# Stores of the edge sort spread over more stages, self loops beside a matrix product, and tables of the last layer in one run per lane

## The chip, the cores and the metric

The kernel runs on one core of one Trainium2 chip. The metric is the device time of one execution in microseconds (us). Engines are named as in the profile: PE is TensorE (matmul), DVE VectorE, ACT ScalarE, POOL GpSimd, SP SyncE, which here only issues transfers.

## What is computed

A graph network on 3125 nodes of 64 features and 100,000 edges that are sorted by target. Four layers follow each other, each as `x = layernorm(x + layer(x))`:

```
x = LN(x + L0(x, edges, 4))            # four normalised sums over neighbours
x = LN(x + L1(x, src, dst, ...))       # edge MLP gives a gate; sum and max per target; node MLP
x = LN(x + L2(x, edges, ...))          # three convolutions with self loops
x = LN(x + L3(x, relations, edges, edge_type))

def L3(e, ...):                        # two hops, head = src, tail = dst
    res = e
    for _ in range(2):
        e = l2_normalize(agg(e, relations, head, tail, type))   # mean over each head's edges
        res = 0.5 * res + e
    return res
```

The last layer sums by source. So the edges must be sorted once more, by source, before it begins.

## The kernel before

Nodes lie as 25 blocks of 128 in the first three layers and as 33 blocks (`SB`) of 96 (`BN`) in the last one. The program is a chain of stages. Each stage is a call of `drive`, which gives every engine its own program, and between two stages stands a barrier of all engines (L111, L113): the next stage begins when the last engine is through, POOL's queue of transfers included (the instruction DRAIN at L111).

**Sorting by source.** `sort_places` computes for each edge its row in the sorted table and keeps rows and edge codes in DRAM as 28 batches of 28 columns (`K.queue`). The 784 stores that carry them out are indirect transfers of 128 edges each, issued by POOL at L445 in `place_batches` and called placements below. SP brings each batch into one of two buffers (`queue_batches`, L430) after waiting until the placements of the batch two before it have landed. The placements of a stage are paced: after every `stored` of them POOL waits for one more increment of `pace`, a semaphore of that stage's own work. They go beside this other work: 224 in the stage that builds the pair matrix (`build_pairs`), 280 in the stage of the first layer's hops (`Pairs.hops`, paced by `full[0]`, 6 at a time), the rest in `dense` calls of later layers and in the second layer's loops.

**Stages around the change**, in the order of time: "steps" and "bases" compute tables of the second layer's edge loop and of node degrees (L516 to L640 and L768 on); then `build_pairs`; then `hops`, where PE and DVE run four rounds over 25 blocks and SP first stores the pair matrix (L1072); then the fetch of weights, the first `dense` of the second layer, and its edge loop. `merge` (L1655 to L1672) joins maximum and sum of the messages on DVE, while POOL adds self loops to the pair matrix (`with_loops`, L862, 25 instructions; they follow the matrix's load). Two `dense` calls of the node MLP follow, the first with batch 18.

**The last layer.** `steps3` turns the sorted edges into lists of ids with matmuls (L1923): DVE prepares `local`, `where`, `half`, `odd` and `kind`, and one semaphore, `selected`, lets PE begin. `edge_loop3` runs once per hop. Its start (`nodes_first`) makes the table `tab3` of 3168 rows of 66 values in SBUF, SP stores it (L2126), and then POOL gathers 68 tiles of tail rows in each of 12 steps (L2158, 1632 gathers in both hops); DVE, ACT and PE work on what was gathered. In the second hop the residual mix is computed at L2430 and stored (L2129). `mix_in` loads it and the layer's input (L2011, L2012), and POOL halves and adds them (L2030, L2033) before DVE's final sum and norm (L2045).

In `by_block`, the layout of both tables before, node n is row n, so that one of the 96 lanes holds rows n, n+96, n+192 and so on: 33 separate runs of 264 bytes for `tab3` and of 256 bytes for `mix`.

## Time and profile before

| what | us |
|---|---|
| runs | 5718.30, 5718.80, 5719.78 (median 5718.8) |
| profiled execution, its own time | 5712.27 |
| its span | 5710.5 |
| busy: DVE, POOL | 3715.3, 3453.4 |
| busy: PE matmul, PE weight load, ACT | 2917.1, 2314.5, 1759.2 |
| POOL: 1632 gathers of the last layer, busy | 1699.1 |
| POOL: 784 placements, busy | 807.9 |

The profile is of one execution. Busy shares are averages over some forty stages with different limits, so they tell little about a change that touches eight of them; the timeline and the waits inside a stage do. In rows of a timeline the first number is the start in us from the span's start, the second the duration; the bracket says how long the engine stood idle before and what released it, and "issue" there is time in which it waited for nothing the profile shows. A row "POOL L445" is a placement's work on POOL, not its landing in DRAM.

### The profile page before, as it was taken

Reading aid. Unit: us, or ns where it says so; the run is one execution under the profiler, and the core shown is the slowest. Engines: PE = TensorE matmul, PEld = TensorE weight load, DVE = VectorE, ACT = ScalarE, POOL = GpSimd, SP = SyncE. Lnnn points to the kernel's source line nnn. Section 1 sums busy time; section 2 is a strip of 40 time slices with the busy share of each in tenths; the row PEclk is TensorE's granted clock in tenths of the full one; section 3 lists DMA queues with packets and bytes.
Section 4 is the critical chain, followed back from the end, with each engine's and each line's share of the span. In section 5 each row is a group of like instructions: output and inputs, shape, how many; then the busy total and the mean of one; then the engine's idle time right before and its main releaser. Section 6 shows DMA issues by size and latency. Waiting matters only on the chain. (4 is left out here: it accounts for less than half of the span.)

```text
span 5710.5 us, 76336 instructions
## 1 busy us (share of the span) xinstructions
PE 2917.1 (51%) x18212; PEld 2314.5 (41%) x18213; DVE 3715.3 (65%) x6539; ACT 1759.2 (31%) x5177; POOL 3453.4 (60%) x3383
## 2 busy tenths in 40 slices
PE   4344578724555555264736426455564244555543
PEld 1233456514454444143424225444453234444443
DVE  4645554306777777233332569899998579998987
ACT  0055500001111111110010035655654146556552
POOL 4077337737777777432613477777772577777771
PEclk7655589956666666566857655556655556665655
DMA  6031040027777777500000212222220321222211
GB/s 214 31 106 52 0 142 2 2 79 205 217 214 221 214 216 203 173 9 0 4 7 9 53 42 58 45 54 50 50 46 7 68 54 44 55 49 50 53 32 18
DMA packets 491952, 449.20 MB, mean 79 GB/s; under 512 B 135374, under 2 KB 439172, under 8 KB 491667
## 3 DMA queue, kind: packets, MB, share of 16 engines
q1 hardware_dynamic: 257963, 232.05, 14.7%
q0 software_dynamic: 116768, 136.51, 10.3%
q10 hardware_dynamic: 116936, 77.08, 4.2%
q8 instruction: 149, 2.44, 0.2%
q14 instruction: 136, 1.11, 0.1%
HBM read 308.22 MB, written 137.16 MB: 78 GB/s over the span
## 5 line engine op out<-in xcount | busy, mean ns | idle before, releaser
L2158 POOL DMA_INDIRECT tg<-tab_d,tail_ids x1632 | 1699.1, 1041 | 543.3 <-issue 494.6
L445 POOL DMA_INDIRECT sorted_edges_d<-place_batch x784 | 807.9, 1030 | 749.6 <-DMA place_batch<-place_queue_d 340.0
L2197 PE MATMUL acc<-msg,sum_hot 128*96 128x65 f32 x3264 | 547.0, 366 | 961.0 <-ACT msg L2271 748.5
L2197 PEld LDWEIGHTS acc<-msg,sum_hot 128*96 128x96 f32 x3264 | 529.4, 279 | 976.9 <-issue 976.9
L1494 POOL DMA_INDIRECT xg<-tab_d,src_i x784 | 767.7, 979 | 252.3 <-issue 238.5
L2187 PE MATMUL hr<-near_table,near_hot 128*128 x4896 | 679.2, 266 | 197.2 <-DVE near_hot L2319 95.0
L2187 PEld LDWEIGHTS hr<-near_table,near_hot 128*128 128x128 f16 x4896 | 497.4, 105 | 380.5 <-issue 281.8
L2246 ACT ACTIVATE pr<-hr 128x396 f32<-128x396 f32 x576 | 277.8, 483 | 590.9 <-PE hr L2187 584.7
L2260 ACT ACTIVATE msg<-tg,coef_b 128x64 f32<-128x64 f32 x1632 | 396.6, 334 | 31.3 <-DVEq L2667 31.3
L1508 PE MATMUL hq<-ex,sameU 128*128 128x128 f32 x1568 | 269.2, 350 | 260.5 <-DVEq L1613 194.4
L2487 DVE TENSOR_REDUCE scal<-prod 128x17 f32<-128x1088 f32 x288 | 370.5, 1286 | 9.9
L1508 PEld LDWEIGHTS hq<-ex,sameU 128*128 128x128 f32 x1568 | 262.3, 265 | 275.8 <-issue 275.8
L2266 ACT ACTIVATE pr<-pr,coef_c 128x64 f32<-128x64 f32 x1496 | 365.4, 334 | 0.0
L717 PE MATMUL ring<-step_cells,step_lows 128*128 128x200 f16 x1184 | 229.6, 374 | 232.3 <-DVE step_lows L695 95.6
L906 PE MATMUL aggps<-shared,pair_m 128*128 128x192 bf16 (+1 forms) x1800 | 263.0, 286 | 80.4 <-DVEq L934 65.8
L717 PEld LDWEIGHTS ring<-step_cells,step_lows 128*128 128x128 f16 x1184 | 174.9, 157 | 287.0 <-issue 286.2
L2311 DVE TENSOR_TENSOR scal<-scal 128x68 f32<-128x68 f32 (+1 forms) x1272 | 264.3, 245 | 28.2 <-ACT scal L2251 9.3
L1611 DVE TENSOR_TENSOR h<-hq,xg 128x1792 f32<-128x1792 f32 x56 | 113.4, 2025 | 212.2 <-DMA xg<-tab_d,src_i 206.8
L695 DVE TENSOR_TENSOR step_lows<-low_rows,room 128x1024 f16<-128x1024 f16 x148 | 102.6, 693 | 222.5 <-PE ring L717 222.1
L906 PEld LDWEIGHTS aggps<-shared,pair_m 128*128 (+1 forms) x1800 | 176.1, 99 | 167.3 <-issue 97.5
L1546 ACT ACTIVATE back<-bk 128x896 f32<-128x896 f32 x112 | 102.8, 918 | 443.2 <-PE bk L1518 443.2
L2311 DVE TENSOR_TENSOR prod<-pr,tg 128x1088 f32<-128x1088 f32 x96 | 124.3, 1295 | 169.4 <-DMA tg<-tab_d,tail_ids 166.5
(469 smaller groups left out, 5402.5 us busy)
## 6 DMA issues: line engine op xcount, KB each, us to landing
ex<-spread_d SPq DMA_DIRECT2D x112, 448.0 KB, 5.5
msg_d<-back ACTq DMA_DIRECT2D x112, 448.0 KB
near_hot<-head_row_d SPq DMA_DIRECT2D x96, 408.0 KB
tg<-tab_d,tail_ids POOLq DMA_INDIRECT x1632
spread_d<-zeros ACTq DMA_DIRECT2D x28, 896.0 KB, 10.9
spread_d<-zeros SPq DMA_DIRECT2D x28, 896.0 KB, 8.8
idsU<-dst_short_d SPq DMA_DIRECT2D x112, 224.0 KB, 6.6
pairs_d<-pair_m SPq DMA_DIRECT2D x3, 4800.0 KB
```

Of the source, the lines that this page charges most:

```text
L445: l.eng.indirect_dma_start(K.sorted_edges[:, :], bass.IndirectOffsetOnAxis(ap=K.batch[:, n % 2, 0, k:k + 1], axis=0), K.batch[:, n % 2, 1, ...
L717: e.matmul(banks[:, bass.ds(regs[k], KW)], lows[s][:, :, k], cells[s][:, k, :], start=False, stop=False, skip_group_check=True).then_inc(s ...
L906: ins = l.eng.matmul(ps[s][:, 0:3 * w], self.m[:, b, bass.ds(at, P)], parts[:, b, :], start=b == 0, stop=b == NB - 1)
L1494: l.eng.indirect_dma_start(xg[j.c % ROWS][:, half * H + k, :], None, K.tab1, bass.IndirectOffsetOnAxis(ap=src_i[:, t:t + 1], axis=0)).then ...
L1508: ins = e.matmul(hq[:, k, :], same[j.slot][:, k, :], ex[j.slot][:, k, :], start=True, stop=True)
L2158: e.indirect_dma_start(tg[:, u % TAILS * GQ + k, :], None, K.tab3, bass.IndirectOffsetOnAxis(ap=K.tail_ids[:, u * GQ + k:u * GQ + k + 1], ...
L2187: ins = e.matmul(hr[(u * FILLS + g) % 2][:, c:c + PW3], near_hot[u % HOTS][:, k, :], rows[:, bass.ds(at[k] + n * PW3, PW3)], start=n == 0, ...
L2197: ins = e.matmul(sums[:, bass.ds(at[k], D + 1)], sum_hot[u % 2][:, k, :], msg[u % QN][:, k, :], start=False, stop=False, skip_group_check= ...
L2260: a.activation(msg[u % QN][:, k, 0:D], tg[:, tails(u).start + k, 0:D], ACT.Copy, scale=kB[s][:, t.start + k:t.start + k + 1]).then_inc(tai ...
L2266: a.activation(r, r, ACT.Copy, scale=kC[s][:, k:k + 1]).then_inc(kinds_scaled, 1)
L2311: tt_ = lambda o, x, y, op: v.tensor_tensor(o, x, y, op).then_inc(l.sem, l.add(1))
L2487: v.tensor_reduce(sc[:, n, q * GQ:(q + 1) * GQ], prod[q % 2][:, :, :], AX.X, ADD).then_inc(l.sem, l.add(1))
```

## The change

1. Placements are spread otherwise. Batch 0 goes into the stage "steps" and batch 1 into "bases", both unpaced; batches 2 to 9 into `build_pairs` as before; batches 10 to 16 into `hops` (196 in place of 280, 4 for each increment), two of them fetched ahead of the pair matrix's stores; batch 17 into the first `dense` of the second layer.
2. `with_loops` leaves `merge` and runs on POOL beside the node MLP's second `dense`; its half identity takes the room of the first `dense`'s weights.
3. `tab3` lies by lane: lane p's 33 rows follow each other, so its store is one run of 8712 bytes per lane. Tail ids are recomputed to match: n becomes (n mod 96)*33 + n div 96, by five more DVE instructions in `steps3`; `selected` is raised twice.
4. `mix` lies by lane too. The second hop halves its value once more and adds half of the input, so that `mix_in` loads one array and needs nothing from POOL.

```
-def place_batches(l, K, first, count, pace, stored):
+def place_batches(l, K, first, count, pace=None, stored=BATCH):
...
-            if done and done % stored == 0:
+            if pace is not None and done and done % stored == 0:
@@ steps
+            place_batches(l, K, 0, 1)
...
+            queue_batches(l, K, 0, 2)
@@ build_pairs
-            place_batches(l, K, 0, 8, turned, 4)
+            place_batches(l, K, 2, 8, turned, 4)
@@ node_bases
+        place_batches(l, K, 1, 1)
@@ Pairs.hops
+                queue_batches(l, self.K, 10, 2)
                 for c0, c1 in self.columns:
                     l.eng.dma_start(cells[:, :, c0:c1], self.m[:, :, c0:c1]).then_inc(kept, 16)
-                queue_batches(l, self.K, 8, 10)
+                queue_batches(l, self.K, 12, 5)
...
-                place_batches(l, self.K, 8, 10, full[0], 6)
+                place_batches(l, self.K, 10, 7, full[0], 4)
@@ second layer
-        dense(nc, K, tabs[:, :, :], [(K.x[:, :, :], wab[:, :])], bab[:, :])
+        dense(nc, K, tabs[:, :, :], [(K.x[:, :, :], wab[:, :])], bab[:, :], batches=(17, 1))
...
-    drive(nc, "merge", dict(vector=vector, gpsimd=gpsimd))
+    drive(nc, "merge", dict(vector=vector))
     dense(nc, K, h2, [(mm, wn1a), (K.x[:, :, :], wn1b)], bn1, relu=True, room=droom, batches=(18, 1))
-    dense(nc, K, o, [(h2, wn2)], bn2, room=droom)
+    dense(nc, K, o, [(h2, wn2)], bn2, room=droom, beside=loops)
@@ steps3, vector
+            v.tensor_scalar(half[:, :, :], tail[:, :, :], 2731, None, ALU.mult).then_inc(l.sem, l.add(1))
+            v.tensor_scalar(odd[:, :, :], tail[:, :, :], SB, None, ALU.mult).then_inc(l.sem, l.add(1))
+            settle()
+            for c in range(QC):
+                v.scalar_tensor_tensor(chosen[:, c, :], steps16[:, :], first[:, c:c + 1], begun[:, c, :], ALU.is_gt, ALU.mult).then_inc(l.sem, l.add(1))
+            settle()
+            v.sem_inc(selected, 1)
+            v.tensor_scalar(half[:, :, :], half[:, :, :], 18, None, ALU.logical_shift_right).then_inc(l.sem, l.add(1))
+            settle()
+            v.scalar_tensor_tensor(tail[:, :, :], half[:, :, :], float(1 - SB * BN), odd[:, :, :], ALU.mult, ALU.add).then_inc(l.sem, l.add(1))
@@ steps3, tensor
+                    if h == 0 and j == 2:
+                        e.wait_ge(selected, 2)
@@ mix_in
-        s.dma_start(mix[:, :, :], by_block(K.mix)).then_inc(loaded, 16)
-        s.dma_start(x[:, :, :], by_block(K.xd)).then_inc(loaded, 16)
+        s.dma_start(x[:, :, :], K.mix.rearrange("p (b f) -> p b f", f=D)).then_inc(loaded, 16)
...
-        l.eng.tensor_scalar(mix[:, :, :], mix[:, :, :], 0.5, None, ALU.mult).then_inc(l.sem, l.add(1))
...
-        l.eng.tensor_tensor(x[:, :, :], x[:, :, :], mix[:, :, :], ALU.add).then_inc(added, 1)
@@ edge_loop3
-        q.dma_start(by_block(K.tab3), tab).then_inc(tails_stored, 16)
+        q.dma_start(by_lane(K.tab3), tab).then_inc(tails_stored, 16)
...
-                v.scalar_tensor_tensor(mix[:, :, :], mix[:, :, :], 0.5, ev, ALU.mult, ALU.add).then_inc(l.sem, l.add(1))
+                v.scalar_tensor_tensor(sq, mix, 0.5, ev, ALU.mult, ALU.add).then_inc(l.sem, l.add(1))
             settle()
             v.sem_inc(heads_tabled, 1)
+            if hop == 1:
+                v.scalar_tensor_tensor(mix, sq, 0.5, mix, ALU.mult, ALU.add).then_inc(l.sem, l.add(1))
+                settle()
+                v.sem_inc(mixed, 1)
```

How the order of instructions moves is shown at three places. The first is POOL from the stage "steps" to the first `dense` of the second layer, the difference in two pieces (`sorted_edges_d` is the sorted table, `place_batch` the two buffers of a batch; L111, L113 and L162 are the barrier and the start of a stage's program):

```order
 L552 IOTA count_f 128x1184
+L445 DMA sorted_edges_d<-place_batch 100352x1 x28
 L111 UNCONDITIONAL_BRANCH
 L113 ISA x2
 L162 UNCONDITIONAL_BRANCH
-L783 IOTA node_ids 128x3208
+L785 IOTA node_ids 128x3208
+L445 DMA sorted_edges_d<-place_batch 100352x1 x28
 L111 UNCONDITIONAL_BRANCH
```

```order
-L445 DMA sorted_edges_d<-place_batch 100352x1 x280
+L445 DMA sorted_edges_d<-place_batch 100352x1 x196
 L111 UNCONDITIONAL_BRANCH
-L113 ISA x8
+L113 ISA x6
 L162 UNCONDITIONAL_BRANCH
```

POOL had nothing but one IOTA in each of the first two stages; now each holds 28 placements behind it, and the stage of the hops holds 84 fewer.

The second is SP in the stage of the hops, before:

```order
L1072 DMA pairs_d<-pair_m 128x25x768 x3
L1072 DMA pairs_d<-pair_m 128x25x832
L430 DMA place_batch<-place_queue_d 128x56 x10
L111 UNCONDITIONAL_BRANCH
```

and of the change:

```order
L430 DMA place_batch<-place_queue_d 128x56 x2
L1076 DMA pairs_d<-pair_m 128x25x768 x3
L1076 DMA pairs_d<-pair_m 128x25x832
L430 DMA place_batch<-place_queue_d 128x56 x5
L111 UNCONDITIONAL_BRANCH
```

Two batches are now fetched ahead of the four stores of the pair matrix, and five behind.

The third is DVE in `steps3`, before:

```order
L1865 TENSOR_SCALAR begun_1<-steps_3_1,last_step_1 112x944 x7
L1866 TENSOR_SCALAR kind_1<-kind_1 112x896
L1867 TENSOR_SCALAR half_1<-tail_1 112x896
L1868 TENSOR_SCALAR odd_1<-tail_1 112x896
L1871 SCALAR_TENSOR_TENSOR chosen_1<-steps_3_1,first_step_1,begun_1 112x944 x7
L1872 TENSOR_SCALAR kind_1<-kind_1 112x896
L1873 CAST half_1<-half_1 112x896
L1874 CAST odd_1<-odd_1 112x896
L1880 TENSOR_TENSOR off_1<-colps_1,count_1 128x408
```

and of the change:

```order
L1877 TENSOR_SCALAR half_1<-tail_1 112x896
L1878 TENSOR_SCALAR odd_1<-tail_1 112x896
L1881 SCALAR_TENSOR_TENSOR chosen_1<-steps_3_1,first_step_1,begun_1 112x944 x7
L1884 TENSOR_SCALAR half_1<-half_1 112x896
L1886 SCALAR_TENSOR_TENSOR tail_1<-half_1,odd_1 112x896
L1888 TENSOR_SCALAR half_1<-tail_1 112x896
L1889 TENSOR_SCALAR odd_1<-tail_1 112x896
L1891 CAST half_1<-half_1 112x896
L1892 CAST odd_1<-odd_1 112x896
L1893 TENSOR_SCALAR kind_1<-kind_1 112x896
L1899 TENSOR_TENSOR off_1<-colps_1,count_1 128x408
```

Before, PE was released behind L1874; now it is released once behind L1881 and a second time, for `half` and `odd`, behind L1893.

## Rows read from the trace of the kernel before

**Rows 1.** Windows: stretch, length, busy PE PEld DVE ACT POOL, PEclk, DMA, GB/s.

```profile
760.00:1117.00 357.00, 320.97 (x2477) 233.79 (x2478) 140.00 (x575) 0.00 (x0) 239.28 (x250) 1.00 0.14 39
1117.00:1170.00 53.00, 0.42 (x6) 0.20 (x3) 14.48 (x24) 0.00 (x0) 32.57 (x31) 0.54 0.02 3
```

**Rows 2.** Timeline of the hops' stage: first and last placement, DVE's end, next stage.

```profile
798.10 0.95 POOL L445 DMA_INDIRECT sorted_edges_d<-place_batch  x1 [170.12 <-DMA place_batch<-place_queue_d]
...
1130.82 1.82 DVE L1135 TENSOR_TENSOR nodes<-nodes,col_b 128x1600 f32<-128x1600 f32 x1
...
1157.76 0.96 POOL L445 DMA_INDIRECT sorted_edges_d<-place_batch  x1 [0.30 <-issue]
1164.95 0.17 DVE L1408 MEMSET bab<- 128x128 f32 x1 [32.31 <-PEq L113]
```

**Rows 3.** Timeline, first dense of the second layer: DVE's eleventh group, next stage's start.

```profile
1209.57 0.69 DVE L1256 TENSOR_TENSOR tabs<-dop,bab 128x512 f32 x1 [2.67 <-PE dop L1240]
...
1216.72 0.18 DVE L1326 TENSOR_SCALAR has<-degree 128x25 f32<-128x25 f32 x1 [1.30 <-PEq L113]
```

**Rows 4.** Timeline, node MLP's first dense: last placement, start of the next stage.

```profile
2450.42 0.96 POOL L445 DMA_INDIRECT sorted_edges_d<-place_batch  x1 [0.30 <-issue]
...
2457.96 0.63 ACT L1213 ACTIVATE spare<-B 128x512 f32 x1 [6.03 <-PEq L113]
```

**Rows 5.** Timeline: POOL's first instruction of the stages bases and build_pairs.

```profile
198.12 2.81 POOL L783 IOTA node_ids<- 128x3208 f32 x1 [53.95 <-SPq L111]
...
274.51 0.30 POOL L669 IOTA cell_row<- 128x200 f32 x1 [73.58 <-POOLq L113]
```

**Rows 6.** Timeline of merge (POOL, DVE), and the start behind the second dense.

```profile
2365.92 17.59 POOL L862 TENSOR_TENSOR pair_m<-pair_m,spare 128x128 f16<-128x128 f16 x18 [0.28 <-POOL spare L1669]
...
2374.67 3.60 DVE L1664 TENSOR_TENSOR B<-B,has_edges 128x3200 f32<-128x3200 f32 x1
...
2386.29 2.60 POOL L862 TENSOR_TENSOR pair_m<-pair_m,spare 128x128 f16<-128x128 f16 x7 [2.78 <-DMA pair_m<-pairs_d]
...
2484.70 1.82 DVE L1678 SCALAR_TENSOR_TENSOR B<-nodes,B 128x1600 f32<-128x1600 f32 x1 [1.29 <-PEq L113]
```

**Rows 7.** Timeline of steps3: an integer operation of two inputs, DVE's last, PE's first.

```profile
3136.41 1.08 DVE L1859 SCALAR_TENSOR_TENSOR local<-block,head 112x896 f16<-112x896 int32 x1
...
3152.82 0.62 DVE L1874 CAST odd<-odd 112x896 f16<-112x896 int32 x1
...
3153.65 2.54 PE L1923 MATMUL colps<-chosen,local 112*128 112x408 f16 x7 [52.58 <-DVEq L1876]
```

**Rows 8.** Timeline, first hop: the table's store and the first gather.

```profile
3209.85 0.32 SPq L2126 DMA_DIRECT2D tab_d<-pr  x1
...
3220.13 0.99 POOL L2158 DMA_INDIRECT tg<-tab_d,tail_ids  x1 [16.30 <-DMA tab_d<-pr]
```

**Rows 9.** Windows of 2 us: the table's store early and late, the mix's store.

```profile
3211.00:3213.00 2.00, 0.00 (x0) 0.00 (x0) 2.00 (x1) 0.00 (x0) 0.00 (x0) 0.50 1.04 189
...
3215.00:3217.00 2.00, 0.00 (x0) 0.00 (x0) 1.97 (x2) 0.00 (x0) 0.00 (x0) 0.50 1.01 86
4472.00:4474.00 2.00, 2.00 (x5) 0.46 (x3) 2.00 (x4) 0.00 (x0) 1.39 (x3) 0.50 0.83 201
```

**Rows 10.** Page's part 5 and waits for tile tg: the gathers, who waited for them.

```profile
L2158 POOL DMA_INDIRECT tg<-tab_d,tail_ids x1632 | 1699.1, 1041 | 543.3 <-issue 494.6
...
  DVE prod L2311: 166.5, 28
```

**Rows 11.** Timeline, second hop: the mix on DVE and the gather beside it.

```profile
4468.89 2.35 DVE L2430 SCALAR_TENSOR_TENSOR pr<-pr 96x2112 f32<-96x2112 f32 x1
4470.02 2.04 POOL L2158 DMA_INDIRECT tg<-tab_d,tail_ids  x1 [0.30 <-issue]
```

**Rows 12.** Timeline of mix_in: POOL's first operation, DVE's start behind its second.

```profile
5677.76 5.55 POOL L2030 TENSOR_SCALAR mix<-mix 96x2112 f32<-96x2112 f32 x1 [41.99 <-DMA x<-x_kept_d]
...
5688.15 1.29 DVE L2045 TENSOR_TENSOR x<-x,e 96x1088 f32<-96x1088 f32 x1 [10.45 <-POOL x L2033]
```

More of the change, by code:

```diff
@@ L471, in keep_common @@
     K.pairs = dr("pairs", [NP * PW, 1], F16)
-    K.xd, K.mix = (dr(n, [NP, D], F32) for n in ("x_kept", "mix"))
+    K.xd, K.mix = dr("x_kept", [NP, D], F32), dr("mix", [BN, SB * D], F32)
     K.tab1, K.qtab = dr("tab1", [NP, D + P], F32), dr("qtab", [NP, P], F32)
@@ L1171, with dense @@
 TH = T // 2
-def dense(nc, K, out, pieces, bias=None, relu=False, room=None, batches=None):
+def dense(nc, K, out, pieces, bias=None, relu=False, room=None, batches=None, beside=None):
     width = out.shape[2]
@@ L1271, in dense @@
             programs.update(sync=sync, gpsimd=gpsimd)
+        if beside is not None:
+            programs.update(gpsimd=beside)
         drive(nc, "dense", programs)
@@ L1639, in finish1 @@
     droom = spare[:, 0:2048]
-    half = spare[:, 0:P // 2].bitcast(F16)
     at = 2048
@@ L1646, in finish1 @@
     wn1a, wn1b, wn2, bn1, bn2, mid = views
+    half = wn1a[:, 0:P // 2].bitcast(F16)
     L, R = slice(0, D), slice(D, P)
@@ L1665, in vector, with loops @@
         l.eng.wait_ge(l.sem, l.done())
-    def gpsimd(l):
-        e = l.eng
-        e.tensor_scalar(half, K.ident[:, :], 0.5, None, ALU.mult).then_inc(l.sem, l.add(1))
-        e.wait_ge(l.sem, l.done())
-        e.sem_inc(l.sink, 1)
+    def loops(l):
+        l.eng.tensor_scalar(half, K.ident[:, :], 0.5, None, ALU.mult).then_inc(l.sem, l.add(1))
+        l.eng.wait_ge(l.sem, l.done())
+        l.eng.sem_inc(l.sink, 1)
         pairs.with_loops(l, half)
-    drive(nc, "merge", dict(vector=vector, gpsimd=gpsimd))
+    drive(nc, "merge", dict(vector=vector))
     dense(nc, K, h2, [(mm, wn1a), (K.x[:, :, :], wn1b)], bn1, relu=True, room=droom, batches=(18, 1))
-    dense(nc, K, o, [(h2, wn2)], bn2, room=droom)
+    dense(nc, K, o, [(h2, wn2)], bn2, room=droom, beside=loops)
     def vector(l):
@@ L1783, in by_block, with by_lane @@
     return rows[0:SB * BN, :].rearrange("(b p) f -> p b f", p=BN)
+def by_lane(rows):
+    return rows.rearrange("(p b) f -> p b f", p=BN)
 def steps3(nc, K):
@@ L1869, in vector @@
             settle()
-            for c in range(QC):
-                v.scalar_tensor_tensor(chosen[:, c, :], steps16[:, :], first[:, c:c + 1], begun[:, c, :], ALU.is_gt, ALU.mult).then_inc(l.sem, l.add(1))
-            v.tensor_scalar(kind16[:, :, :], kind[:, :, :], float(BN), None, ALU.add).then_inc(l.sem, l.add(1))
             v.tensor_copy(half16[:, :, :], half[:, :, :]).then_inc(l.sem, l.add(1))
             v.tensor_copy(odd16[:, :, :], odd[:, :, :]).then_inc(l.sem, l.add(1))
+            v.tensor_scalar(kind16[:, :, :], kind[:, :, :], float(BN), None, ALU.add).then_inc(l.sem, l.add(1))
             settle()
@@ L1920, in tensor @@
                 for j, xs in enumerate(((local16,), (where16,), (half16, half16, odd16))):
+                    if h == 0 and j == 2:
+                        e.wait_ge(selected, 2)
+                        e.sem_inc(l.sink, 1)
                     for n, x in enumerate(xs):
@@ L2002, in mix_in @@
     sb = lambda n, s, d: st.enter_context(nc.sbuf_tensor(fresh(n), s, d))
-    e, sq, x, mix = (sb(n, [BN, SB, D], F32) for n in ("e3", "sq3", "x3", "mix3"))
+    e, sq, x = (sb(n, [BN, SB, D], F32) for n in ("e3", "sq3", "x3"))
     counts = sb("counts3", [BN, SB], F32)
     mean, var = sb("mean3", [BN, SB], F32), sb("var3", [BN, SB], F32)
-    loaded, squared, added, centred, mixed, stored = (st.sem(fresh(n)) for n in ("loaded", "squared", "added_x", "centred", "mixed", "stored"))
+    loaded, squared, centred, mixed, stored = (st.sem(fresh(n)) for n in ("loaded", "squared", "centred", "mixed", "stored"))
     halves = [slice(0, 17), slice(17, SB)]
@@ L2025, in scalar @@
             l.eng.activation(sq[:, at, :], x[:, at, :], ACT.Square).then_inc(squared, 1)
-    def gpsimd(l):
-        l.eng.wait_ge(loaded, 32)
-        l.eng.sem_inc(l.sink, 1)
-        l.eng.tensor_scalar(mix[:, :, :], mix[:, :, :], 0.5, None, ALU.mult).then_inc(l.sem, l.add(1))
-        l.eng.wait_ge(l.sem, l.done())
-        l.eng.sem_inc(l.sink, 1)
-        l.eng.tensor_tensor(x[:, :, :], x[:, :, :], mix[:, :, :], ALU.add).then_inc(added, 1)
     def vector(l):
@@ L2041, in vector @@
         entities(v, l, acc, e, sq, squared, counts[:, :], a, b, t)
-        v.wait_ge(added, 1)
+        v.wait_ge(loaded, 16)
         for at in halves:
@@ L2061, in vector @@
         v.wait_ge(mixed, 2)
-    drive(nc, "mix", dict(sync=sync, scalar=scalar, gpsimd=gpsimd, vector=vector))
+    drive(nc, "mix", dict(sync=sync, scalar=scalar, vector=vector))
 def edge_loop3(nc, K, st, table, relation, acc, hop):
@@ L2101, in edge_loop3 @@
     keyed = [st.sem(fresh(f"keyed{r}")) for r in range(HOTS)]
-    squared, rooted, kinds_last = sem("squared"), sem("rooted"), sem("kinds_last")
+    squared, rooted, kinds_last, mixed = sem("squared"), sem("rooted"), sem("kinds_last"), sem("mixed3")
     (shaped, cleared, near_made, near_full, near_taken, coefs, tails_scaled, kinds_scaled, summed, positive, sum_made, added, asked, answered) = (
@@ L2125, in sync @@
         q.wait_ge(tails_tabled, 1)
-        q.dma_start(by_block(K.tab3), tab).then_inc(tails_stored, 16)
+        q.dma_start(by_lane(K.tab3), tab).then_inc(tails_stored, 16)
         if hop == 1:
-            q.wait_ge(heads_tabled, 1)
-            q.dma_start(by_block(K.mix), mix).then_inc(mix_stored, 16)
+            q.wait_ge(mixed, 1)
+            q.dma_start(K.mix.rearrange("p (b f) -> p b f", f=D), mix).then_inc(mix_stored, 16)
         for u in range(HOTS, QUARTERS):
```

3 lines of the change are left out of this document (2 added, 1 removed).

## The prediction

> **What bounds the kernel now.** I read the busy shares first, to see that no engine is full throughout, and then the kernel stage by stage: since a barrier ends each stage, what counts is which engine comes last in it. The windows show the hops' rounds bound by PE (320.97 us of 357, POOL 239.28), and then 53 us in which PE works 0.42, DVE 14.48 and POOL 32.57 [rows 1]: POOL alone holds the stage. The timeline says how long: DVE's last instruction ends at 1132.64, the last placement at 1158.72, and the next stage starts at 1164.95 [rows 2], 6.23 after it, since POOL's queue is drained before the barrier. Where DVE ends a stage, the next starts 1.30 later [rows 3]. So three stages end with POOL's work while DVE is through: the hops, `merge` and `mix_in`. In the last layer POOL is the pace: its 1632 gathers take 1699.1 us and it stands idle 543.3 around them, of which 494.6 is the 0.30 of issuing each; the rest is mostly the wait for each hop's table (16.30 in the first [rows 8]). DVE waits for gathered rows 166.5 us [rows 10]. What starts the gathers earlier therefore ends the hop earlier.
>
> **The change part by part**, against the profiled execution's 5712.27 us.
>
> *The hops' stage.* 84 of 280 placements leave it. Before, the first one ran at 798.10, after 170.12 idle for its batch, since the fetch stood behind the pair matrix's stores on SP [rows 2]. Now two batches are ahead of these stores, and 196 placements at 4 for each increment need 49 groups. The increments come about every 6.87 us (357 us by 52 of them), four placements cost 4 x 1.26 = 5.0 (0.96 and 0.30 each [rows 2]), so POOL waits for each increment and places its last group near 760 + 48 x 6.87 = 1090, ends near 1095 and is drained near 1100. That is before DVE, which ends at 1132.64 as it did, so the next stage starts at 1132.64 + 1.30 = 1133.94 and not at 1164.95: **-31.0**. Bounds: -31.0, and -24 if the end of DVE comes later because POOL's stores now crowd the start, which the trace speaks against (PE and not DVE is the bound there, DVE 140.00 of 357 [rows 1]).
>
> *The first dense of the second layer* takes 28 of them, 4 after each of 6 increments of `done[0]`. The sixth comes with the eleventh group, whose sum on DVE starts at 1209.57 [rows 3]. The last four placements end near 1209.4 + 5.1 = 1214.5. Then comes the drain: 6.23 from the last placement to the next stage in the hops [rows 2], 6.58 in the one dense that already has a batch (2451.38 to 2457.96 [rows 4]). That gives 1220.8 in place of 1216.72: **+4.2**. Bounds 0 (the drain is hidden) and +6 (the placements lag one group).
>
> *Steps and bases* take 28 placements each. POOL's next instruction after the first comes at 198.12, after 53.95 idle, and after the second at 274.51, after 73.58 idle [rows 5]. 28 placements cost 28 x 1.26 = 35.3, or 28 x (1.93 + 0.30) = 62 if each ran as slowly as a gather beside a two-input DVE operation (2.04 [rows 11]). With 6.2 for the drain this is 41.5 or at worst 68: in bases it fits into the 73.6 idle, in steps 41.5 fits into 53.95 and 68 doesn't, but the two-input operations of DVE fill a small part of that stage. I take **0**, bounds 0 and +6; without that cover the cost would be 41.5 a stage. The pair matrix's stage keeps its 224 placements: 0.
>
> *merge.* DVE ends at 2378.27, POOL's additions at 2388.89, because the last seven wait for the matrix's load [rows 6]. Without them the stage ends with DVE: **-10.5**, bounds -9 and -11.5. They cost 17.59 for 18 beside DVE and 2.60 for 7 alone [rows 6], so 10 to 25 us with the half identity, beside a dense that runs from 2457.96 to 2484.70 less the barrier, 25.4 us [rows 4, 6]. They fit, and the load has landed by then: 0, bound +1. Batch 18 is now fetched some 10 us earlier, beside the end of the matrix's load; its placements are paced by the dense, which hides a late start unless it is over 5 us.
>
> *steps3.* PE starts at 3153.65, 0.2 behind DVE's last of `kind`, `half` and `odd` (0.62 each, overlapping to 1.6 in all [rows 7]). These now stand behind the release: **-1.6**. The new chain (0.62, 1.08, 1.15 for `half` and `odd`, 1.7 for the casts and `kind`, by [rows 7]) takes some 4.6, and PE has `local` with 2.54 and `where` with about as much before it needs them. Bounds -1.6 and +0.5.
>
> *The tables.* The store is issued at 3209.85 and the first gather starts at 3220.13, after 16.30 idle for it [rows 8]. The data flow at 189 GB/s at first and at 86 near the end, while the mix's rows of 256 bytes ran at 201 [rows 9]. At 201 the 0.84 MB need 4.2 us and not the 6.2 that I read; one run per lane should do no worse and may do better, 3 us. I take **-3.2 in each hop**, nearer to the fast row since the tail at 86 goes, bounds 0 and -5. In the Trainium skill, "DMA: Bandwidth & Descriptors", Specifications, full rate wants transfers of at least 512 bytes. By that the mix's 256-byte rows should be as slow as the table's 264, and [rows 9] show them at over twice the late rate, so the measurement decides and the gain may be smaller than the rule suggests.
>
> *The second hop's extra operation* costs 2.35 on DVE like the one at L2430, which DVE wins back while it waits for gathers. The gather beside that one took 2.04 where another took 0.99 [rows 8, 11]: **+1.1** on POOL. Bounds 0 and +2.4.
>
> *mix_in.* POOL begins at 5677.76, as the second load lands. DVE is ready at 5688.15 - 10.45 = 5677.70 and waits 10.45 for POOL's two operations [rows 12]. These go. The stage's loads begin about 10 us earlier, so one load with half of the bytes lands before DVE is ready: **-10.4**, bounds -8 and -10.5.
>
> SP's two more fetches in steps stand ahead of the loads of that stage: +0.3.
>
> **Sum**: -31.0 + 4.2 - 10.5 - 1.6 - 3.2 - 3.2 + 1.1 - 10.4 + 0.3 = -54.3, so 5712.3 becomes 5658.0. The median of the runs lies 6.5 above the profiled execution, and the next runs are as likely to lie there: 5718.8 - 54.3 = **5664.5**. About 0.2%, 11.4 us, is what a measurement of this kernel tells from no change.
>
> **Rivals.**
>
> *The gathers become slower (the other side).* They are the pace of 24 steps, so what each gains in length counts 1632 times. To be slower than before by 0.2% the 54.3 must be lost and 11.4 more: 65.7 / 1632 = 0.040 us each, from a mean of 1.041 to 1.081 [rows 10]. If they came to 1.09, the time would be 5664.5 + 80 = 5745. For it: the table's rows lie in another order, and a gathered tile's rows with it. Against it: the duration on POOL is that of writing descriptors, whose number and size stay, and ids are random in either layout. Chance 3%.
>
> *POOL holds back DVE in the two early stages.* A placement writes descriptors while DVE runs operations of two inputs; the rows show the gather delayed (2.04) and DVE's 2.35 unchanged [rows 11]. If it went the other way, each of 14 long operations of the two stages would wait up to one placement, 0.96: +13, 5678. In the Trainium skill, "GPSIMD Engine Reference", Key points, POOL shares its memory interfaces with DVE in such operations; it speaks against putting stores there, but doesn't say who wins. The trace so far has DVE winning. With the case that POOL outlasts steps (+6, 5670.5) chance 12%.
>
> *The table's store doesn't get faster.* Its late rate could come from something else, such as queues that finish at different times. Then 6.4 are missing: 5671. Chance 20%.
>
> *The hops' gain doesn't come in full.* If the increments come later than I read, or the batches 12 to 16 still wait behind the pair matrix's stores, POOL lags. 112 placements behind a first one at 798 need only 141 us, so it would have to lag by over 30 us more than before. If it did, half of the 31 would be missing: 5680. Chance 5%.
>
> **How the numbers follow.** The forecast has 60%, within it 5655 to 5672 by the bounds of the dense (-4 to +2), the tables (-4 to +6) and the early stages. The rivals at 5671 and 5678 belong to the faster side too. For 8 in 10 I reach from 5652 to 5680. Faster by over 0.2% holds the forecast and the last three rivals, less 2 in 100 for a slowing of the gathers that only eats the gain: 0.95; same 0.02, slower 0.03 from the first rival.
>
> **What would show it.** Right: the next stage behind the hops starts 1.3 us after DVE's last instruction, with POOL's last placement near 1095; `merge` ends with DVE; the idle time before the first gather shrinks from 16.30 by some 3 us; DVE in `mix_in` has no wait of 10 us; the first dense's next stage starts some 4 us later. Wrong: gathers of a mean above 1.05, a stage steps or bases that ends with POOL, placements still running past 1132, or a table store that takes as long.

## The result and the profile after

| what | before | changed |
|---|---|---|
| runs, us | 5718.30 to 5719.78, median 5718.8 | 5662.21, 5667.17, 5668.14, median 5667.17 |
| profiled execution, us | 5712.27 | 5667.17 |
| ratio of the runs, 95% interval | | 0.9915 [0.9902, 0.9929] |

The kernel became 51.6 us faster by the medians, against 54.3 forecast (5664.5). The profiled executions differ by 45.1: that of before lay 6.5 below its kernel's median, that of the change on it. What follows is worked out between these two, stage by stage, and then tested.

The page of the changed kernel (span, busy times, and the two groups of part 5 that concern the change):

```profile
span 5665.4 us, 76347 instructions
...
PE 2926.1 (52%) x18212; PEld 2321.6 (41%) x18213; DVE 3718.3 (66%) x6544; ACT 1759.1 (31%) x5177; POOL 3474.6 (61%) x3381
...
L2171 POOL DMA_INDIRECT tg<-tab_d,tail_ids x1632 | 1713.4, 1050 | 532.9 <-issue 495.6
L445 POOL DMA_INDIRECT sorted_edges_d<-place_batch x784 | 834.0, 1064 | 858.9 <-DMA place_batch<-place_queue_d 352.4
```

The averages say little: the engines' busy shares moved by a hundredth at most. One number matters later: the gathers take 1.050 us in the mean and not 1.041 [rows 10], which is 14.3 us over all 1632 (1713.4 against 1699.1).

| stage | forecast, us | by the two timelines, us |
|---|---|---|
| to the end of "steps" | +0.3 | +3.25 |
| "bases", `build_pairs` | 0 | +0.2, +1.5 |
| the hops' stage | -31.0 | -30.5 |
| first dense of the second layer | +4.2 | +1.75 |
| `merge` | -10.5 | -11.2 |
| node MLP's two dense calls | 0 | -0.3 |
| steps3 to PE's first matmul | -1.6 | -1.7 |
| table, first and second hop | -3.2, -3.2 | -5.0, -5.5 |
| from first gather to the end of the hop, first and second | 0, +1.1 | +3.0, +10.6 |
| `mix_in` | -10.4 | -10.35 |

What is missing to -45.1 is about -1 in stages that the change doesn't touch.

**The hops** (timeline of the changed kernel: last placement, DVE's last instruction, next stage's first):

```profile
1098.46 0.96 POOL L445 DMA_INDIRECT sorted_edges_d<-place_batch  x1 [0.31 <-issue]
...
1135.71 1.83 DVE L1139 TENSOR_TENSOR nodes<-nodes,col_b 128x1600 f32<-128x1600 f32 x1
1139.38 0.17 DVE L1414 MEMSET bab<- 128x128 f32 x1 [1.84 <-PEq L113]
```

The last placement ends at 1099.42, 38 us before DVE, and the next stage starts 1.84 behind DVE; before, it started 6.2 behind the last placement [rows 2]. The whole tail of POOL is gone. The stage itself began 4.9 later than before.

**The first dense** (last placement, DVE's last, next stage):

```profile
1188.51 0.95 POOL L445 DMA_INDIRECT sorted_edges_d<-place_batch  x1 [0.30 <-issue]
1189.52 0.42 DVE L1260 TENSOR_TENSOR tabs<-dop,bab 128x256 f32<-128x256 f32 x1 [1.38 <-PE dop L1244]
...
1192.98 0.18 DVE L1332 TENSOR_SCALAR has<-degree 128x25 f32<-128x25 f32 x1 [3.04 <-PEq L113]
```

DVE ends at 1189.94, and the next stage starts 3.04 behind it instead of 1.30 [rows 3]. POOL's last placement ended at 1189.46, so 3.5 us pass between it and the next stage, not the 6.2 to 6.6 that I forecast. The 6.58 of [rows 4] was a misreading. In that dense, too, four placements stood at the end behind a pause, but DVE had one more operation to do:

```profile
2454.24 1.83 DVE L1261 TENSOR_SCALAR B<-B 128x3200 f32<-128x3200 f32 x1
```

It ended at 2456.07, and the next stage started 1.89 behind it: DVE ended that stage, and the 6.58 is no price of POOL's. By the records of the instruction DRAIN itself, POOL was through 4.63 us after the last placement in the hops of the kernel before, and 2.48 after it in that dense; in the new dense it is 2.36. A drain isn't a fixed price: here it was longer behind the long unbroken row of stores than behind four.

**Steps** (SP's last load, DVE's first operation on loaded data, DVE's last, next stage):

```profile
149.66 2.01 SPq L566 DMA_DIRECT2D before_i<-in_dst_dram  x3
...
156.35 0.63 DVE L574 TENSOR_SCALAR group_i<-step_raw 112x896 int32<-112x896 int32 x1 [11.17 <-DMA before_i<-in_dst_dram]
...
199.42 0.55 DVE L620 SCALAR_TENSOR_TENSOR room<-stepps,count_f 1x392 int32<-1x392 f32 x1
201.37 2.81 POOL L785 IOTA node_ids<- 128x3208 f32 x1 [16.66 <-SPq L111]
```

Before, DVE's first operation on loaded data came earlier:

```profile
153.29 0.63 DVE L572 TENSOR_SCALAR group_i<-step_raw 112x896 int32<-112x896 int32 x1 [8.31 <-DMA before_i<-in_dst_dram]
```

DVE waits 11.17 us for the last load, and 8.31 before. Everything behind is shifted by that: from that operation to DVE's last it takes 43.6 us, and 43.4 before, and its seven `chosen` operations take 9.63 in both kernels. POOL's placements didn't slow DVE; the loads landed later. How much later varies: e3 and e4 below have the same early stages, and there the wait was 9.29 and 8.76.

**merge and the loops** (DVE's last of `merge`, the next stage's first, and POOL's additions in their new place):

```profile
2351.34 3.49 DVE L1670 TENSOR_TENSOR B<-B,has_edges 128x3200 f32<-128x3200 f32 x1
...
2355.91 0.42 ACT L1217 ACTIVATE spare<-B 128x256 f32 x1 [67.52 <-PEq L113]
...
2424.36 7.70 POOL L865 TENSOR_TENSOR pair_m<-pair_m,spare 128x128 f16<-128x128 f16 x20 [0.28 <-POOL spare L1674]
```

DVE now ends `merge` (2354.83), and the 25 additions run beside the second dense in 9.5 us altogether; the dense takes 26.9 us, and 26.7 before [rows 6].

**steps3** (PE's first, DVE's last conversion, PE's first matmul on `half`):

```profile
3115.57 2.54 PE L1945 MATMUL colps<-chosen,local 112*128 112x408 f16 x7 [50.89 <-DVEq L1883]
...
3119.57 0.62 DVE L1893 TENSOR_SCALAR kind<-kind 112x896 f16<-112x896 int32 x1
...
3120.39 3.03 PE L1945 MATMUL colps<-chosen,half 112*128 112x408 f16 x14
```

PE starts 4.6 us ahead of the end of DVE's chain, which is done at 3120.19, just before PE needs it at 3120.39. The margin is 0.2 us.

**The tables** (the store and the first gather of hop one, the first gather of hop two; then the first two windows of 2 us of the store, columns as in [rows 9]):

```profile
3171.99 0.30 SPq L2139 DMA_DIRECT2D tab_d<-pr  x1
...
3177.26 1.19 POOL L2171 DMA_INDIRECT tg<-tab_d,tail_ids  x1 [11.28 <-DMA tab_d<-pr]
...
4413.07 1.25 POOL L2171 DMA_INDIRECT tg<-tab_d,tail_ids  x1 [24.78 <-DMA tab_d<-pr]
```

```profile
3173.00:3175.00 2.00, 0.00 (x0) 0.00 (x0) 2.00 (x1) 0.00 (x0) 0.00 (x0) 0.50 0.97 274
3175.00:3177.00 2.00, 0.00 (x0) 0.00 (x0) 1.97 (x2) 0.00 (x0) 0.00 (x0) 0.50 0.19 78
```

The wait falls from 16.30 to 11.28 [rows 8]. The data flow at 274 GB/s in the first of these windows and are through in the second; the slow end at 86 [rows 9] is gone. **mix_in** (the one load, and DVE's sum, which waits for nothing; it came at 5688.15 behind a wait of 10.45 [rows 12]):

```profile
5632.59 0.30 SPq L2033 DMA_DIRECT2D x<-mix_d  x1
...
5643.03 1.29 DVE L2058 TENSOR_TENSOR x<-x,e 96x1088 f32<-96x1088 f32 x1
```

### The profile page after: what moved, and what is told of

It is laid out like the page before. It is cut to its first block and busy times, and to the rows that moved or that the text cites. A ratio compares the mean times of both kernels' runs of the same rounds, so it can differ in the third digit from the quotient of the medians.

```text
span 5665.4 us, 76347 instructions
## 1 busy us (share of the span) xinstructions
PE 2926.1 (52%) x18212; PEld 2321.6 (41%) x18213; DVE 3718.3 (66%) x6544; ACT 1759.1 (31%) x5177; POOL 3474.6 (61%) x3381
## 5 line engine op out<-in xcount | busy, mean ns | idle before, releaser
L2171 POOL DMA_INDIRECT tg<-tab_d,tail_ids x1632 | 1713.4, 1050 | 532.9 <-issue 495.6
L445 POOL DMA_INDIRECT sorted_edges_d<-place_batch x784 | 834.0, 1064 | 858.9 <-DMA place_batch<-place_queue_d 352.4
```

The costliest lines, as they stand in the source:

```text
L445: l.eng.indirect_dma_start(K.sorted_edges[:, :], bass.IndirectOffsetOnAxis(ap=K.batch[:, n % 2, 0, k:k + 1], axis=0), K.batch[:, n % 2, 1, ...
L2171: e.indirect_dma_start(tg[:, u % TAILS * GQ + k, :], None, K.tab3, bass.IndirectOffsetOnAxis(ap=K.tail_ids[:, u * GQ + k:u * GQ + k + 1], ...
```

## The experiments

Theory: each part brings what its stage shows, and the 9 us by which the profiled execution misses the forecast (45.1 against 54.3) lie in the gathers. Rivals: the layout by lane makes gathers slower; the added operation does; or hops vary from run to run. All kernels start from the changed one. Runs on one chip are compared with each other; e1 to e4 ran on one (there the kernel before took 5706.28 to 5718.59, median 5714.13, 9 runs), e5 to e8 and e9 to e12 on two others.

### e1: the stores of the sort as before

```
-            place_batches(l, K, 0, 1)
...
-            queue_batches(l, K, 0, 2)
...
-        place_batches(l, K, 1, 1)
...
-            place_batches(l, K, 2, 8, turned, 4)
+            place_batches(l, K, 0, 8, turned, 4)
...
-                queue_batches(l, self.K, 10, 2)
...
-                queue_batches(l, self.K, 12, 5)
+                queue_batches(l, self.K, 8, 10)
-                place_batches(l, self.K, 10, 7, full[0], 4)
+                place_batches(l, self.K, 8, 10, full[0], 6)
...
-        dense(nc, K, tabs[:, :, :], [(K.x[:, :, :], wab[:, :])], bab[:, :], batches=(17, 1))
+        dense(nc, K, tabs[:, :, :], [(K.x[:, :, :], wab[:, :])], bab[:, :])
```

> The spread of the sort's stores is undone, all else is as in the change. Theory A (POOL's tail alone held the hops' stage; the early stages pay 4.6 us, of which 3.1 is the later landing of a load in the stage steps, and the first dense 1.8): 30.5 - 4.6 - 1.8 = 24 us slower than the change, near 5691, with 5 us less before the hops' stage and the next stage 31 us behind DVE's end again. Theory B (stores are better spread because the memory queues are less crowded in the hops): more than 35 us slower. If the last layer's gathers keep their 1.050 us here, the spread of stores has nothing to do with their slowing.

Measured: 5693.71 (5685.05 to 5696.81), ratio 0.9962 [0.9949, 0.9976] to the kernel before, against 0.9915 for the change: 0.47%, some 27 us. The next stage behind the hops starts behind POOL again:

```profile
1165.30 0.17 DVE L1410 MEMSET bab<- 128x128 f32 x1 [33.57 <-PEq L113]
```

The stage took 425.7 us (424.6 before), steps and bases were back at 57.0 and 76.3, `build_pairs` at 465.8, the dense at 44.86. Here "steps" is counted from the stage's first instruction to the next stage's first; the kernel before has 57.4, the change 60.4. So the spread of stores is worth 30.5 - 1.75 - 4.7 = 24, as theory A says. It alone pays ahead of the hops, but not always 4.7: on this chip the hops began at 739.6 (e1) and 740.0 (e2) without it, and at 742.7 (e3) and 741.1 (e4) with it.

### e2: ten batches in the hops, two of them fetched ahead

```
-                queue_batches(l, self.K, 10, 2)
+                queue_batches(l, self.K, 8, 2)
...
-                queue_batches(l, self.K, 12, 5)
+                queue_batches(l, self.K, 10, 8)
-                place_batches(l, self.K, 10, 7, full[0], 4)
+                place_batches(l, self.K, 8, 10, full[0], 6)
```

with steps, bases and the first dense as in e1.

> All ten batches stay in the hops' stage as before the change, 6 for each increment, but two are fetched ahead of the pair matrix's stores; steps, bases and the first dense have none. Theory A (what held the hops was the first placement's start at 798, not the number: 280 x 1.26 = 353 us from about 762 end at 1115, drained near 1120, ahead of DVE's end): 6 us faster than the change, near 5661, since steps and the first dense give their 4.6 and 1.8 back. Theory B (with every increment used up the placements run past DVE's end at 1132.6, because a collision with DVE's norm or a late batch costs them more): within 10 us of the change on either side, POOL last in the stage.

Measured: 5663.43 (5655.85 to 5666.58), ratio 0.9911 [0.9897, 0.9924]. The last placement and the next stage:

```profile
1113.30 0.96 POOL L445 DMA_INDIRECT sorted_edges_d<-place_batch  x1 [0.30 <-issue]
...
1134.56 0.17 DVE L1411 MEMSET bab<- 128x128 f32 x1 [1.85 <-PEq L113]
```

280 placements are done at 1114.26, 18 us before DVE. The stage took 394.6, as with the change (394.1), and the early stages and the dense had their times of before. e1 and e2 differ in nothing but the place of this fetch, and their medians lie 30.3 us apart. So on this chip what held the hops was the late first placement, 170 us idle for a batch behind the pair matrix's stores, and not the number of stores. Whether fewer stores without the earlier fetch are enough as well wasn't tried here. On this chip one line on SP's queue is worth as much as the whole spread. As a time a gain over the change isn't shown: the intervals overlap.

### e3: the table by block; e4: the mix as before

e3 takes `by_block(K.tab3)` and the ids, DVE's order and the single release of before; e4 takes `mix_in` of before and

```
-                v.scalar_tensor_tensor(sq, mix, 0.5, ev, ALU.mult, ALU.add).then_inc(l.sem, l.add(1))
+                v.scalar_tensor_tensor(mix[:, :, :], mix[:, :, :], 0.5, ev, ALU.mult, ALU.add).then_inc(l.sem, l.add(1))
...
-            if hop == 1:
-                v.scalar_tensor_tensor(mix, sq, 0.5, mix, ALU.mult, ALU.add).then_inc(l.sem, l.add(1))
-                settle()
-                v.sem_inc(mixed, 1)
```

> The last layer's table by block as before, ids unconverted, the rest as in the change. Theory A (store and steps3 gave 5.0 + 5.5 + 1.7, and the gathers' 1.050 against 1.041 us is a pattern of collisions that has nothing to do with the layout): 12 us slower than the change, near 5679, gathers anywhere between 1.04 and 1.055. Theory B (rows by lane make the gathers slower, 0.009 x 1632 = 14 us): gathers back at 1.041, time within 4 us of the change.

> The residual mix as before: two arrays loaded at the end, halved and added on POOL, no second operation on DVE in the second hop. Theory A (10.4 at the end, 1.1 on the gathers of the second hop): 9 us slower than the change, near 5676. Theory B (the added operation on DVE shifts the steps against the gathers and is what made the second hop 10.6 us longer): about as fast as the change, and the second hop's 816 gathers span 1097 us as before the change in place of 1108.

Measured: e3 5675.99 (5674.14 to 5680.66), ratio 0.9940 [0.9926, 0.9953]; e4 5666.44 (5652.46 to 5671.60), ratio 0.9922 [0.9908, 0.9936]. e3 loses what its stages say: the first gathers come 9.2 and 9.3 us behind their stores, not 5.3 and 5.2, PE's first matmul in steps3 comes 1.5 later, and `mix_in` keeps its gain. Its gathers did not return to 1.041: the mean was 1.050 and 1.045 in the two hops. The layout isn't what slows them. e4 is the surprise. At `mix_in` it loses its gain (DVE waits 10.85 us for POOL again), yet its median is that of the change. The rows of tile `tg` (minimum, median, maximum in ns) show why, for the kernel before, the change, e3 and e4:

```profile
L2158 POOL DMA_INDIRECT tg<-tab_d,tail_ids x1632: 940/944/2970, 3220.1 to 5555.9; - x182
```

```profile
L2171 POOL DMA_INDIRECT tg<-tab_d,tail_ids x1632: 942/952/2807, 3177.3 to 5521.5; - x182
```

```profile
L2159 POOL DMA_INDIRECT tg<-tab_d,tail_ids x1632: 942/952/2764, 3183.3 to 5528.3; - x182
```

```profile
L2180 POOL DMA_INDIRECT tg<-tab_d,tail_ids x1632: 940/944/2819, 3166.7 to 5496.0; - x182
```

The median gather takes 944 ns before and in e4, 952 in the change and in e3 (also in e1 and e2). All 1632 together took 1699.1 us before and 1697.7 in e4, but 1713.4 in the change and 1709.5 to 1716.3 in e1 to e3. So some 14 us are lost, but the step of the median isn't all of it: of the gathers up to 1.1 us the mean moved by 3 ns only, from 966 to 969, which is less than 5 us; the rest lies in those over 1.1 us (343.9 us before, 361.3 in the change, eight more of them). Both theories for e4 fell as put: the second hop is not alone (its 816 gathers spanned 1098.8 us, the first hop's 1093.7; with the change 1108.4 and 1100.0), and the price isn't 1.1 us. By these profiles the new mix gives 10.35 at the end and takes about as much in the gathers of both hops. In times that isn't settled: e4's interval also holds the 9 us of theory A. And its profiled execution was the fastest of its five, 14 us below their median; its first gather came 10.6 us earlier than the change's, in stages that are the same in both. One of them, the second layer's edge loop, took 1048.0 us in the change and 1041.2 in e4.

### e5 to e8: a second chip

e5 is the change itself, e6 the kernel of e2, e7 moves the two fetches of "steps" behind the stage's loads, and e8 undoes both e3's and e4's parts.

```
         def sync(l):
             e = l.eng
-            queue_batches(l, K, 0, 2)
...
                 e.dma_start(out, ends(t0, t1), allow_slow_non_contiguous=True).then_inc(loaded, 16)
+            queue_batches(l, K, 0, 2)
```

> The change itself, run beside the next three. The profiles so far show each stage within 0.5 us of its price but the 1632 gathers between 1094 and 1108 us a hop. Theory A (the length of a hop varies from execution to execution, whatever the kernel): the two hops' gathers come out differently from the 1100 and 1108 of the change's first profile, by up to 8 us, and the rest of the stages the same within 1 us. Theory B (the change's layout or its second operation sets it): again 1100 and 1108 within 2 us.

> The kernel with ten batches in the hops, two of them fetched ahead, once more beside the change. Its stages promise 4.6 + 1.8 = 6.4 us less than the change. Theory A (the stages add up): 4 to 8 us below the change in the medians. Theory B (variation of the hops hides it): within 3 us.

> In the stage steps the two batches are fetched behind the stage's own loads instead of ahead of them. Theory A (the 3.1 us of that stage are the last load's landing, late because fetches and placements share the memory queues with it): DVE's first shift on loaded data starts 8.3 us after its cast, as before the change, and the stage is 3 us shorter; POOL ends near 190 and is drained before DVE is through. Theory B (placements slow DVE's own operations): the stage stays 3 us longer than before the change. Theory C (POOL now outlasts the stage): 1 to 5 us longer than the change.

> The last layer is as before the change in all its parts (table by block, ids unconverted, mix by two inputs), the early stages as in the change. By the stages 5.0 + 5.4 + 1.7 + 10.3 - 1.1 = 21.3 us slower than the change, less what the gathers gain. Theory A (variation of executions): gathers of a hop span anything from 1094 to 1108. Theory B (the change's last layer makes them slower): both spans within 1 us of 1097, and the kernel only 7 to 10 us slower than the change.

| kernel | median, us | to the kernel before (7547.02, 11 runs) |
|---|---|---|
| e5, the change | 7382.83 | 0.9786 [0.9766, 0.9806] |
| e6, ten ahead | 7457.81 | 0.9898 [0.9873, 0.9923] |
| e7, loads first | 7390.01 | 0.9793 [0.9774, 0.9813] |
| e8, last layer as before | 7407.91 | 0.9817 [0.9797, 0.9836] |

This chip runs every kernel a third slower. DVE's, ACT's and POOL's instructions last as long as on the first; the loops' engines stand idle more, in time that the profile puts to "issue" or to a release it doesn't show. Gathers no longer set the pace there, so the spans of 816 say nothing and the theories for e5 can't be told apart. Three readings hold all the same. In e7 DVE's first operation on loaded data waits 8.44 us for its loads, in e5 10.30:

```profile
152.50 0.63 DVE L574 TENSOR_SCALAR group_i<-step_raw 112x896 int32<-112x896 int32 x1 [8.44 <-DMA before_i<-in_dst_dram]
```

```profile
154.62 0.63 DVE L574 TENSOR_SCALAR group_i<-step_raw 112x896 int32<-112x896 int32 x1 [10.30 <-DMA before_i<-in_dst_dram]
```

Fetching behind the loads gives the stage its early start back, as before the change (8.31). Yet the stage became 10 us longer: 69.2 against 58.8 in e5. DVE waited twice, 6.4 and 8.3 us, for results of PE (the profile names no releaser), and PE's weight loads came mostly one at a time, each behind a pause in which it waited for nothing that the profile shows:

```profile
191.88 0.10 PEld L634 LDWEIGHTS stepps<-chosen,cell 112*128 112x128 f16 x1 [1.18 <-issue]
...
194.01 0.10 PEld L634 LDWEIGHTS stepps<-chosen,where 112*128 112x128 f16 x1 [1.29 <-issue]
```

This lasted until about 197.5, as POOL's placements (the last ended at 194.7) and its drain (197.5) did. So none of the three theories is right: the load was earlier, but neither the 3 us came back nor did POOL end the stage. e8 is 25 us slower than the change by the medians; its last layer has the old waits again (the first gather, and DVE's sum behind POOL):

```profile
3677.26 0.99 POOL L2168 DMA_INDIRECT tg<-tab_d,tail_ids  x1 [15.34 <-DMA tab_d<-pr]
...
7383.67 1.29 DVE L2055 TENSOR_TENSOR x<-x,e 96x1088 f32<-96x1088 f32 x1 [10.42 <-POOL x L2043]
```

and the old median of a gather, 944 ns, where e5 to e7 have 947 to 952:

```profile
L2168 POOL DMA_INDIRECT tg<-tab_d,tail_ids x1632: 938/944/3054, 3677.3 to 7182.8; - x182
```

Third, e6 is 75 us slower than the change, where theory A had it 4 to 8 us faster, and its hops' stage took 514 us against 412.

### e9 to e12: a third chip

e9 is the change, e10 the kernel of e2, e11 that of e7, and e12 is the change with the hops' fetches behind the pair matrix's stores:

```
-                queue_batches(l, self.K, 10, 2)
                 for c0, c1 in self.columns:
                     l.eng.dma_start(cells[:, :, c0:c1], self.m[:, :, c0:c1]).then_inc(kept, 16)
-                queue_batches(l, self.K, 12, 5)
+                queue_batches(l, self.K, 10, 7)
```

> The change once more, beside the next three. On the second chip all kernels took some 1700 us more, in idle time that the records put to issue or to no releaser. Theory A (that belongs to the chip): if this is a chip like the first, 5660 to 5670, stages as in its first profile within 1 us, and the two spans of 816 gathers again different, between 1094 and 1108. Theory B (the layout by lane makes gathers slow): 1100 and 1108 again.

> Ten batches in the hops, two fetched ahead. On the first chip its hops' stage took 394.6 us like the change's 394.1, on the second chip 514 against 412, because the increments that pace it came every 9.6 us. Theory A (stages add up on a chip like the first): 6 us below the change. Theory B (the hops' rounds suffer from placements at every increment wherever instruction supply is short): hops' stage over 400 us again.

> Batches fetched behind the loads of the stage steps. On the second chip DVE waited 8.4 us for its loads, as before the change (8.3), and not 10.3, but other idle time hid what it brought. Theory A (late landing is all of the 3.1 us): stage back at 55.1 us in place of 58.1, kernel 3 us below the change. Theory B (POOL's drain then ends the stage): 57 to 60 us.

> The change with its hops' fetches behind the pair matrix's stores, as before: seven batches from a first placement near 800. Theory A (either fewer batches or an earlier fetch is enough): 196 placements, 4 for each increment left, start at 800, catch up at 1.26 each (247 us back to back) and end before 1100; the next stage starts 1.3 to 1.9 us behind DVE, same as the change within 0.5 us in this stage. Theory B (the fetch ahead is what did it): the stage longer by 5 us or more.

| kernel | median, us | to the kernel before (7545.65, 11 runs) | hops' stage, us |
|---|---|---|---|
| e9, the change | 7375.89 | 0.9774 [0.9759, 0.9789] | 412.2 |
| e10, ten ahead | 7474.54 | 0.9905 [0.9889, 0.9920] | 510.6 |
| e11, loads first | 7395.25 | 0.9803 [0.9783, 0.9824] | 411.9 |
| e12, seven behind | 7415.41 | 0.9818 [0.9802, 0.9835] | 442.8 |

This chip was like the second, so the theories that counted on one like the first can't be judged. Of e10's theories B holds (510.6 us for the hops), and in e12 the stage is 30 us longer, as in its theory B. In all of them DVE ended the stage of the hops, so POOL's tail isn't what differs; the rounds themselves are slower. The waits of PE between 820 and 1140 (total us, times, longest) for e9 and for e10:

```profile
PEld hopps L991 <- issue: 58.4, 102, 3.4
...
PE hopps L991 <- issue: 30.9, 52, 3.3
```

```profile
PEld hopps L988 <- issue: 107.2, 141, 4.5
...
PE hopps L988 <- issue: 72.5, 105, 1.8
```

With six placements for each increment PE stands idle nearly twice as long for want of nothing that is recorded. That isn't all: the stage's 2500 matmuls were busy 330.7 us at a mean granted clock of 0.93 in e9, and 358.1 at 0.83 in e10, so 27 of the 98 us are a lower clock. In e12 the stage is 30 us longer as well, and this falls beside the back-to-back row of placements with which it catches up: its second two hundred matmuls took 63 us, those of e9 30. On the first chip the change and e2 had the same stage within 0.5 us. So on two of three chips the number of placements beside a round counts, and the change's 4 for each increment is worth some 100 us over 6; the kernel before, which has 6 too and has no profile there, is slower than the change by 2.1% and 2.3% on these two chips. e11 showed the earlier load again (DVE waited 8.56 us for it, 10.70 in e9), and again a longer stage: 69.1 us against 59.7, with the same pauses of PE. Why a placement holds up PE's and DVE's instruction streams on these chips stays open.

## Why the prediction was right, and where its steps were off

The forecast was 5664.5 in a range of 5652 to 5680, and the median came to 5667.17. By its own steps:

- **The hops' stage, -31.0.** Right, mechanism and size: -30.5, DVE ends the stage, POOL's last placement came at 1098.5 where I had written 1095. e2 adds that on this chip the earlier fetch alone does it.
- **The first dense, +4.2.** Mechanism right, size off: +1.75. The step that failed is the drain of 6.2 to 6.6, carried over from a stage with hundreds of placements and from [rows 4], where DVE and not POOL ended the stage; here it was 3.5 with the barrier. The bounds of 0 and +6 held it.
- **Steps and bases, 0 and +0.3.** Too low by 4.7, with `build_pairs`, in this execution. I looked for the cover of POOL's time only and found it. What wasn't covered was the landing of the stage's last load: DVE waited 8.8 to 11.6 us for it in the seven profiles with fetches and placements ahead of it, 8.2 to 8.8 in the five with none, and 8.4 and 8.6 with the fetches behind the loads (e7, e11). Whether the fetches or the earlier placements delay it wasn't told apart, since placements wait for the fetch. Another 1.5 us are in `build_pairs`, on the first chip in every kernel with the new spread (467.1 to 467.4) and in none without it (465.8 to 465.9); its cause wasn't tried.
- **merge, -10.5.** Right: -11.2, and the loops hide beside the second dense.
- **steps3, -1.6.** Right: -1.7, with 0.2 us to spare.
- **The tables, -3.2 each.** Mechanism right, size off: -5.0 and -5.5, of which e3 shows 3.9 and 4.1 as the layout's (its own stores took 9.2 to 9.3, where before they took 10.3 and 10.7). I took the flow of the mix's 256-byte rows, 201 GB/s, as the aim, and single runs reached 274. The Trainium skill, "DMA: Bandwidth & Descriptors", Specifications, says that a full rate wants transfers of at least 512 bytes. By that rule the table's gain was to be expected in full, and the runs agree for the table (86 at the end of its store in rows of 264 bytes, 274 in single runs). The mix doesn't fit it: in rows of 256 bytes it reached 245 in its best window of 2 us before, and by lane, in one run per lane, 251.
- **The second hop's operation, +1.1.** The largest error of the sum: the two hops came out 13.6 us longer. The gather beside the added operation took what I had priced, 2.19 us:

```profile
4431.50 2.35 DVE L2447 SCALAR_TENSOR_TENSOR pr<-pr 96x2112 f32<-96x2112 f32 x1
4432.49 2.19 POOL L2171 DMA_INDIRECT tg<-tab_d,tail_ids  x1 [0.30 <-issue]
```

What failed is that I put the change's effect on all other gathers at nothing in the sum, and left it to my first rival. What e4 and e8 show is that it comes with the new mix: the median gather is 944 ns in the three profiles without it, on a faster and on a slower chip, and 947 to 952 in the eleven with it. No instruction of the new mix runs in the first hop, so it isn't the operation. Nor is it the additional semaphore, which e4 and e8 declare in the loop as the change does. What else that part changes (the size of the array `mix` in DRAM, which e4 and e8 have as before, the order of DVE and SP in the second hop, POOL's program in `mix_in`) wasn't tried one by one; the cause is open.
- **mix_in, -10.4.** Right: -10.35.

Errors of both signs met: the tables and the dense gave 6.5 us more than forecast, the early stages and the gathers took 17. The median still came out within 3 us of the forecast, because the stages were priced on a profiled execution 6.5 below the median of its kernel, which the change's was not: single executions of one kernel lay up to 19 us apart (e4), so an agreement within 3 us is partly luck. Between the two profiled executions the forecast misses by 9.2. The rival of slower gathers, given 3%, was the right place and the wrong size: 9 ns of the 40 that it needed. The rival in which POOL holds back DVE didn't occur: DVE's seven long operations in steps kept their 9.63 us. It was POOL that waited: beside those seven a placement mostly took 1.05 us, and the one beside the next two, on integers, 3.60 in place of 0.96, while they kept their 1.09 and 1.08.

A kernel with e2's fetch order and the old mix wasn't run. On the first chip neither part was shown to lose time against the change, and on the other two chips e2's share would cost 75 to 99 us.

## What to carry to other kernels

When one engine's tail holds a barrier, look first at when its work began: moving two small fetches ahead of the pair matrix's stores on the same queue was worth as much on one chip as that together with moving 84 stores elsewhere. When work is moved under an idle engine, check what it does to that stage's loads and to the other engines, not only the engine's own idle time: the cure of e7 gave the load back and lost 10 us at PE. And an operation that runs 1632 times should be compared by its sum and its median before and after every change around it: 9 ns in the mean took back some 14 us, more than the 10 us gain that the timeline showed plainly.

## What the runs showed that I had not expected

- The kernel before took 5714 us on one chip and 7546 on two others. In the change's profiles DVE's, ACT's and POOL's instructions last as long on either, and more idle time is put to "issue". There PE's rounds slow down with the density of POOL's indirect stores (hops' stage 412, 443 and 511 us for 4 to an increment, for a late start that catches up, and for 6); on the first chip 4 and 6 made no difference (394.1 and 394.6).
- The wait from a table's store to its first gather was 8.9 to 10.7 us in rows of 264 bytes and 5.2 to 5.3 in runs of 8712.
- The drain behind indirect stores isn't constant: 6.2 us with the barrier behind a dense row of them, 3.5 behind four.
- On the two slower chips PE's instructions came singly for some 10 us beside an unbroken row of placements (e7, e11), in a stage that has no such pause when the placements begin 10 us earlier.
